# First turn of a fused two-layer block: absolute sums ahead of the queries, two ternary weights ahead of the row maxima, the third ahead of the attention rows

## The reference, cut to what matters

```python
x = x + tanh(g_xattn[0]) * attention(layernorm(x), ctx, ctx)   # wq, wk, wv, wo; own keys and context keys
x = x + tanh(g_ffn[0])   * ternary_ffn(layernorm(x))           # w1, w3, w2
x = x + tanh(g_xattn[1]) * wkv_recurrence(w, u, layernorm(x), ctx)
x = x + tanh(g_ffn[1])   * moe(layernorm(x))                   # a shared part and the 2 best of 8 experts
```

```python
def ternary_quant(w):
    s = jnp.mean(jnp.abs(w))
    return jnp.clip(jnp.round(w / s), -1.0, 1.0) * s
h1, h3 = x @ w1q.T, x @ w3q.T
out = (silu(h1) * h3) @ w2q.T
```

## Time and profile before

| | us |
|---|---|
| time, median of 3 runs | 754.02 (752.9 to 755.68) |
| the profiled execution, its own time | 754.42 |
| its span, from first to last instruction | 752.7 |
| TensorE busy in the span | 710.4 (94%) |
| VectorE busy | 518.3 (69%) |
| ScalarE busy | 362.0 (48%) |
| GpSimd busy | 331.6 (44%) |
| granted TensorE clock, mean | 0.995 of full speed |

### The profile page before, as it was taken

How to read it: one execution, slowest core, us unless ns; L and a number is a source line. 1 busy time by engine, 2 the same in 40 slices (tenths; PEclk the granted TensorE clock), 3 DMA queues, 4 the chain that set the end, 5 groups by cost and what they waited for, 6 DMA issues and landing times.

```text
span 752.7 us, 13056 instructions
## 1 busy us (share of the span) xinstructions
PE 710.4 (94%) x4612; PEld 592.0 (79%) x4612; DVE 518.3 (69%) x926; ACT 362.0 (48%) x693; POOL 331.6 (44%) x345
## 2 busy tenths in 40 slices
PE   7988978999999999999999999999999999898896
PEld 6776767788878888788877888787877888687786
DVE  4589396775977478774877478874777568799532
ACT  4746625654356535654365535553466444533321
POOL 2005204444538155443537155352637255276364
PEclk9999999999999999999999999999999999999999
DMA  8050000110111011110012011110012010011111
GB/s 290 7 163 33 1 29 1 58 43 29 49 51 58 15 43 57 57 42 14 27 58 83 14 42 56 56 42 14 28 56 79 19 39 30 12 60 43 57 57 56
DMA packets 31875, 37.04 MB, mean 49 GB/s; under 512 B 2958, under 2 KB 23140, under 8 KB 31844
## 3 DMA queue, kind: packets, MB, share of 16 engines
q1 hardware_dynamic: 31844, 36.63, 15.3%
HBM read 32.30 MB, written 4.33 MB: 49 GB/s over the span
## 4 chain that ended last, share of the span: by engine, by line
PE 63%; DVE 13%; issue 4%; POOL 4%; ACT 2%; DVEq 0%; POOLq 0%; ACTq 0%
PE sums L490 16%; PE gate_ps L490 15%; PE up_ps L490 13%; PE transit L490 7%; PE transit L567 3%; PE transit L482 2%; POOL act_sb L1182 2%; POOL hid_l L1173 2%; PE transit L577 2%; PE transit L597 1%; DVE act_sb L1423 1%; DVE act_sb L1421 1%; DVE bn_w L1363 1%; DVE wk L1456 1%; PE transit L621 1%
## 5 line engine op out<-in xcount | busy, mean ns | idle before, releaser
L1173 POOL TENSOR_TENSOR hid_l<-act_sb,hid_h 128x512 fp32r<-128x512 f32 x120 | 164.0, 1367 | 205.3 <-ACT hid_h L971 204.9
L1421 DVE SCALAR_TENSOR_TENSOR act_sb<-act_sb,gate_ps 128x512 f32<-128x512 f32 (+1 forms) x128 | 86.7, 677 | 112.9 <-ACT act_sb L953 112.9
L971 ACT ACTIVATE hid_h<-act_sb 128x512 fp32r<-128x512 f32 (+1 forms) x128 | 80.3, 627 | 116.0 <-POOL act_sb L1182 80.1
L1182 POOL TENSOR_TENSOR act_sb<-act_sb,late 128x512 f32<-128x512 f32 x64 | 97.4, 1523 | 61.5 <-DVE act_sb L1423 59.8
L490 PE MATMUL sums<-down_h,hid_h 128*128 128x256 f32 x320 | 91.9, 287 | 3.9 <-POOL hid_l L1173 3.9
L490 PE MATMUL sums<-down_h,hid_l 128*128 128x256 f32 x320 | 89.9, 281 | 0.0
L490 PE MATMUL sums<-down_l,hid_h 128*128 128x256 f32 x320 | 89.8, 281 | 0.0
L1423 DVE TENSOR_TENSOR act_sb<-act_sb,up_ps 128x512 f32<-128x512 f32 x120 | 82.4, 687 | 4.1
L953 ACT ACTIVATE act_sb<-gate_ps 128x512 f32<-128x512 f32 x80 | 47.2, 590 | 76.6 <-PE up_ps L490 67.5
L490 PEld LDWEIGHTS sums<-down_h,hid_h 128*128 128x128 f32 x320 | 60.3, 188 | 11.0 <-issue 8.3
L490 PE MATMUL gate_ps<-zm_h,gate_h 128*128 128x512 f32 x140 | 60.0, 429 | 9.4 <-DVE act_sb L1423 9.4
(11 more groups left out here) (204 smaller groups left out, 1638.2 us busy)
## 6 DMA issues: line engine op xcount, KB each, us to landing
late<-combine_rows SPq DMA_DIRECT2D x64, 256.0 KB, 3.1
ctx_tok<-in_ctx SPq DMA_DIRECT2D x8, 512.0 KB, 4.1
xa<-in_x SPq DMA_DIRECT2D x7, 512.0 KB, 3.5
out_x<-late SPq DMA_DIRECT2D x7, 512.0 KB, 3.0
wk<-in_L_ffn_w SPq DMA_DIRECT2D x2, 682.0 KB
late<-in_L_ffn_w_down SPq DMA_DIRECT2D x1, 1024.0 KB, 7.6
wk<-in_L_ffn_w_gate SPq DMA_DIRECT2D x2, 512.0 KB, 4.6
wk<-in_L_ffn_w_up SPq DMA_DIRECT2D x2, 512.0 KB, 4.4
```

The source lines that it names most:

```text
L971: nc.scalar.activation(hid_h[0:n, pos], act_sb[0:n, pos], ACT.Copy).then_inc(hid_h_set, 1)
L1173: nc.gpsimd.tensor_tensor(hid_l[:, pos], act_sb[:, pos], hid_h[:, pos].bitcast(F32), ALU.subtract).then_inc(hid_l_set, 1)
L1182: nc.gpsimd.tensor_tensor(act_sb[:, pos], act_sb[:, pos], comb_sb[:, pos], ALU.mult).then_inc(weighted, 1)
L1421: nc.vector.scalar_tensor_tensor(mine, mine, 1.0, gate_ps[pos][0:hidden_rows(chunk)], ALU.add, ALU.mult).then_inc(gated_one, 1)
```

## The change

In turn 0 only:

- TensorE: abs_sums moves from behind the scores to ahead of context_out.
- ScalarE: the absolute sum of w2 moves from behind context_out to ahead of queries, with its two waits.
- VectorE: ternary_scales loses its two gains (gain_m, gain_f), which become a function of their own, gate_gains. The scales and ternary weights 0 and 1 move ahead of row_max. Behind row_scale stand gate_gains and ternary weight 2, which moves from behind shift_done. fade_rows stays behind the wait for shift_done.

No instruction is added or taken away.

```diff
@@ TensorE, turn
                 values(t)
+                if t.fixed and t.i == 0:
+                    abs_sums()
                 context_out(t)
                 m_down(3)
                 scores(t)
-                if t.fixed and t.i == 0:
-                    abs_sums()
@@ ScalarE, turn
                 m_chunk(4)
+                if first:
+                    act.wait_ge(tern_in, 64)
+                    act.wait_ge(low_set, SPLITS["wv"])
+                    nc.scalar.activation(spare2, raw2, ACT.Abs, accum_out=abs_sum[:, 2:3]).then_inc(abs_w2_set, 1)
                 queries(t)
                 own_keys(t)
                 values(t)
                 context_out(t)
                 if first:
-                    act.wait_ge(tern_in, 64)
-                    act.wait_ge(low_set, SPLITS["wv"])
-                    nc.scalar.activation(spare2, raw2, ACT.Abs, accum_out=abs_sum[:, 2:3]).then_inc(abs_w2_set, 1)
                     act.wait_ge(consts_in, 80)
@@ VectorE
             def ternary_scales():
-                dve.wait_ge(gains_set, 1)
-                nc.vector.tensor_scalar(gain_m[:], gains[:, 3:4], 0.5, None, ALU.mult)
                 dve.wait_ge(abs_all, 1)
...
                 nc.vector.tensor_scalar(s_prod[:, 0:1], scales[:, 0:1], scales[:, 1:2], scales[:, 2:3], ALU.mult, ALU.mult).then_inc(tern_chain, 1)
+
+            def gate_gains():
+                dve.wait_ge(gains_set, 1)
+                nc.vector.tensor_scalar(gain_m[:], gains[:, 3:4], 0.5, None, ALU.mult)
                 dve.wait_ge(tern_chain, 2)
                 nc.vector.tensor_scalar(gain_f[:], s_prod[:, 0:1], gains[:, 2:3], 0.5, ALU.mult, ALU.mult)
@@ VectorE, turn
+                if first:
+                    ternary_scales()
+                    ternary_weights(0, 1)
                 row_max(t)
                 m_gate(5)
                 row_scale(t)
                 if first:
-                    ternary_scales()
-                    ternary_weights(0, 1)
+                    gate_gains()
+                    ternary_weights(2)
                 if w:
                     quotient(t, 0)
                 add_attention(t)
@@ VectorE, turn
                 if first:
                     dve.wait_ge(shift_done["A"], t.count("A", 2, 2))
-                    ternary_weights(2)
                     fade_rows()
```

## The result

| | before | after |
|---|---|---|
| time, median of 13 runs, us | 754.32 | 751.00 |
| ratio of after to before | | 0.9945, 95% interval 0.9929 to 0.9961 |
| span of the profiled execution, us | 752.7 | 749.5 |
| granted TensorE clock, mean | 0.995 | 0.995 |

Forecast were 750.0 us and a ratio of 750.0 / 754.02 = 0.9947. The measured ratio compares the two sets of 13 runs with each other; the quotient of their two medians alone is 0.9956.

What follows compares the result with a forecast made beforehand. TensorE bounds the steady turns; in the first turn VectorE's ternary work holds up the first feed-forward matmul. The steps move that matmul from 51.01 to 47.02, 3.99 us earlier: 754.02 - 4.0 = 750.0 us, range 748.5 to 752.3.

Steps and rivals of the forecast that it cites:

- Step 1: ScalarE, first turn: the absolute sum of w2 ends by 17.4, ahead of the query copy at 17.67; cost zero.
- Step 2: TensorE, first turn: the sums matmul in front of context_out delays the scores by 0.21, upper bound 0.36.
- Steps 3 to 6: First turn: row_max at 30.87 behind ternary block, row sums 33.34, products 34.63, add_attention 36.69, z1T 44.19 with fading rows free.
- Step 7: First turn, z1T to first feed-forward matmul: plain chain of 2.83 instead of 4.04, provided TensorE keeps the full clock.
- The clock rival: TensorE's clock falls at the first turn's z1T, giving 751.2, or in the second turn, losing up to 1.2; chance 0.10.
- two signs of being wrong: From the first turn on: query copies after 17.7, ternary steps over 5.6, a clock fall, a later stage not keeping 4.0.

Runs made afterwards that it cites:

- e6: Changed kernel with the ternary steps split and spread over VectorE's waits, and 26 filler products instead of 30 ahead of the first turn's z1T; 749.21 us, ratio 0.9923.
- e2: Changed kernel with ternary weight 2 put back behind the row factors; 751.23 us, ratio 0.9939 to the kernel before.
- e3: Kernel before with only ternary weight 2 moved ahead of add_attention; 757.02 us, ratio 1.0019.
- e4: Kernel before with 42 filler products instead of 30 ahead of z1T in the first turn; 754.96 us, ratio 0.9988.
- e1: Kernel before with only the absolute sum of w2 and the sums matmul moved to the front, VectorE's order unchanged; 755.23 us, ratio 1.000.
- e9: Changed kernel with the experts' down weights loaded ahead of the ternary weights; 752.35 us, ratio 0.9953 to the kernel before.
- e5: Changed kernel without the mark on the row factors ahead of the fading rows; 751.89 us, ratio 0.9953 to the kernel before.

## Why the prediction was right, and where it was off

The steps, counted from the first q matmul (forecast: its times less 15.96):

| step | forecast | measured |
|---|---|---|
| 2: context products, later by | 0.21 | 0.11 |
| 3: row_max | 14.91 | 14.71 |
| 3: row sums | 17.38 | 17.23 |
| 5: add_attention | 20.73 | 20.55 |
| 6: z1T | 28.23 | 28.05 |
| 7: z1T to ff | 2.83 | 2.78 |
| ff | 31.06 | 30.83 |

- Step 1 held: the absolute sum of w2 started at 15.32 and left ScalarE idle 1.21 ahead of the first query copy at 18.11.
- Step 2 was sized too high. Both ends of the range, 0.21 and 0.36, came from a row where the sums matmul stood behind a wait; in the stream of other matmuls it cost 0.11. It also started 0.10 earlier than forecast and took 0.28 in place of 0.36, so VectorE's scales start at 25.31 - 16.40 = 8.91, where step 2 gives 25.05 - 15.96 = 9.09. That 0.18 is nearly all that row_max gained on the forecast; from the scales to row_max it took 5.80, forecast 5.82.
- Steps 3 to 6 held: row_max stands behind the ternary block and delays the softmax, the probabilities come after the softmax, the third weight still holds add_attention (e6 shows the 1.1 that it gives away), and the fading rows are free.
- Step 7 held, and its condition mattered: e2, e3 and e4 show that neither VectorE nor the clock alone gives the short chain. The prediction named both and put the old 4.04 down to VectorE's work; that is half of it. In e3 the same chain is 4.03 with VectorE free.
- The clock rival happened in the profiled execution, at two places: at the second turn's z1T, where I put it (106 to 110 us, 0.60 behind y_T, where I allowed up to 1.2), and at its context products, where I didn't, for 1.68. By the prediction's own list two signs of being wrong came: the clock fell, and y_T kept 2.54 of the 4.22. The chance of 0.10 rested on the idles of 3.15 and 2.83 alone. The trace of the kernel before held a third row that bears on it, the fall after an idle of 1.91 late in the span, and I had not read that far.
- That the profiled span is still near the forecast is partly luck: it lost 0.44 by the later start and 1.68 and 0.60 by the clock, and gained 1.56 because the late fall of the kernel before was absent.
- No load and no mark after ff absorbed the gain: ff to y_T is 61.85 to 61.89 in seven kernels of the table, before and after the change. The four others are the two with a fall at the context products (after, e4), e1 and e9, whose extra 0.45 and 0.23 are told above. The lowest of the 13 times before is 752.85, of the 13 after 748.99: 3.86 apart, near the 4.22 of the trace.
- The median came out 1.0 above the forecast of 750.0, inside the range, with 0.3 of it on the side of the kernel before, whose median over more runs is 754.32. The difference of the medians is 3.32, where the forecast had 4.0.

How often the clock falls in which place was not settled: one trace per kernel shows where, the other runs only a mean.

## What to carry to other kernels

One-time work belongs into waits, and a wait is best read by its two ends: what the engine could start with, and who needs it back. Cut such work into pieces that fit the waits; moved whole, it ended in front of two other steps here and gave away 1.1 us of what it could gain. Where two causes end at the same time, test each alone before a gain is put down to one of them. Before a fall of the clock is given a chance, look for every fall in the whole span, not only in the turns that the change touches.

## What the runs showed of the hardware

- The first q matmul started anywhere from 15.8 to 20.48 us in the ten profiles of kernels whose work up to there is the same (e9 loads in another order). ScalarE's split of wk, which waits for its load alone, started at 6.23 before, 6.89 after and 8.33 in e3. In e2 and e3, the two with the latest q matmul, the granted clock was also at 0.50 from 12 to 14 us. Counting from the first matmul takes these differences out.
- TensorE's granted clock fell after an idle of 3.15, stayed after 2.83 in the same execution, and fell after 2.82 in the kernel after. Late in the span it fell after 1.91 before and stayed after 1.90 in the kernel after. At the context products it fell in the kernel after, behind an idle of 0.95 and 2 us of transposes with two small matmuls; before, behind the same work and an idle of 0.96, it stayed. So idles of these lengths can go either way.
- What a fall costs depends on who waits: 1.68 at the context products, 0.60 behind z1T, where TensorE had 0.85 to spare, and 1.56 late in the span.
- GpSimd's power took 1.22 in place of 1.01 beside VectorE's fading rows (e5). The Trainium skill ("SBUF — State Buffer", section "SBUF: two separate sides") says that VectorE and GpSimd share a pair of ports as a lock, which VectorE takes only in a mode that uses two ports or with two inputs in SBUF, and that the loser waits for the whole instruction. The run agrees in that they get in each other's way; the delay of 0.21 is less than one fading instruction of about 0.44 (0.88 for two), and which instruction waited for which it doesn't show.
